# Value products in four parts, and three groups of transposes moved later, in a fused attention and feed-forward kernel

## The reference, cut to what matters

```python
x = x + attn(layernorm(x), ctx, ctx)     # x, ctx: 16 x 256 x 256
x = x + ffn(layernorm(x))

# attn, 8 heads of 32; gates from [q, k, v] @ ifgate_w.T, soft-capped by 15 * tanh(pre / 15)
lf = cumsum(log_sigmoid(f_pre))
log_d = lf[t] - lf[s] + i_pre[s], causal
d = exp(log_d - max_s log_d)
s_mat = (q @ k.T / sqrt(32)) * d
h = (s_mat @ v) / (max(|sum_s s_mat|, exp(-m)) + 5e-5)
h = h * rsqrt(mean(h * h) + 1e-6) * (1 + outnorm_w)

# ffn, ternary weights with a scale for each output
h = silu(x @ w1) * (x @ w2)              # 256 -> 1024
h = gelu(h @ h1); h = gelu(h @ h2)       # 1024 -> 1024, twice
y = h @ w3                               # 1024 -> 256
```

## Time and profile before

| what | value |
|---|---|
| median of 3 runs | 898.24 us (898.09 to 901.56) |
| the profiled execution | 900.49 us |
| its span, first to last instruction | 898.8 us |
| mean granted TensorE clock | 0.929 of 2.4 GHz |
| busy in the span: TensorE products | 827.8 us |
| weight loads | 703.6 us |
| VectorE | 562.0 us |
| ScalarE | 380.5 us |
| GpSimd | 67.1 us |

### The profile page before, as it was taken

The page is one execution under the profiler, slowest core; times in us unless marked ns, Lnnn a source line. Parts: engine busy times, 40 slices in busy tenths (PEclk is TensorE's granted clock), DMA queues, the critical chain, the costliest instruction groups (busy, mean ns, idle before and its releaser), DMA issues.

```text
span 898.8 us, 11800 instructions
## 1 busy us (share of the span) xinstructions
PE 827.8 (92%) x4610; PEld 703.6 (78%) x4610; DVE 562.0 (63%) x1336; ACT 380.5 (42%) x551; POOL 67.1 (7%) x54
## 2 busy tenths in 40 slices
PE   5447799999999999999999999999999999999777
PEld 5347688887887888888887888888888888888566
DVE  4475585847856584848676594848675673655651
ACT  2230362455534472455535462445435551354131
POOL 4240000200020000200020000100020000000000
PEclk7556898999999999999999998999999999999888
DMA  6573100021001300031003100030012100023740
GB/s 243 230 284 128 69 24 25 24 95 71 24 25 60 129 24 25 24 119 47 24 25 117 72 24 25 24 131 35 24 48 95 47 1 1 24 71 113 211 145 25
DMA packets 14635, 66.40 MB, mean 74 GB/s; under 512 B 2032, under 2 KB 2416, under 8 KB 11504
## 3 DMA queue, kind: packets, MB, share of 16 engines
q1 hardware_dynamic: 13280, 54.07, 17.2%
q0 software_dynamic: 1296, 11.53, 3.3%
HBM read 57.08 MB, written 8.52 MB: 73 GB/s over the span
## 4 chain that ended last, share of the span: by engine, by line
PE 53%; DVE 30%; ACT 6%; DMA 5%; issue 4%; POOL 1%; DVEq 0%; ACTq 0%; POOLq 0%
PE ps_f L1129 11%; PE ps_f L1130 10%; DVE decay L735 8%; PE ps_a L1068 7%; PE ps_f L1105 7%; PE ps_f L1106 7%; DMA decay<-w_cols 5%; PE ps_f L1160 3%; PE ps_f L1159 3%; DVE h_lo L844 2%; DVE decay L751 2%; PE ps_a L1049 2%; DVE decay L868 2%; DVE rms L796 2%; DVE stats L646 1%
## 5 line engine op out<-in xcount | busy, mean ns | idle before, releaser
L1129 PE MATMUL ps_f<-h_hi,wgt 128*128 128x512 f32 x1024 | 415.1, 405 | 6.6 <-DVE h_lo L844 6.6
L1130 PE MATMUL ps_f<-h_lo,wgt 128*128 128x512 f32 x1024 | 409.9, 400 | 0.0
L1129 PEld LDWEIGHTS ps_f<-h_hi,wgt 128*128 128x128 f32 x1024 | 199.6, 195 | 51.1 <-DVE h_lo L844 7.7
L1130 PEld LDWEIGHTS ps_f<-h_lo,wgt 128*128 128x128 f32 x1024 | 199.4, 195 | 40.9
L558 ACT ACTIVATE work<-ps_f,scl 128x512 f32<-128x512 f32 x128 | 87.5, 684 | 242.3 <-PE ps_f L1130 242.1
L844 DVE TENSOR_TENSOR h_lo<-work,h_hi 128x512 fp32r<-128x512 f32 x128 | 86.2, 689 | 145.1 <-ACT h_hi L563 144.0
L1105 PE MATMUL ps_f<-h_hi,wgt 128*128 128x512 f32 x256 | 101.4, 396 | 0.0
L1106 PE MATMUL ps_f<-h_lo,wgt 128*128 128x512 f32 x256 | 100.3, 392 | 0.0
L545 ACT ACTIVATE work<-ps_f,scl 128x512 f32<-128x512 f32 x64 | 44.1, 689 | 92.7 <-PE ps_f L1106 92.7
L563 ACT ACTIVATE h_hi<-work 128x512 fp32r<-128x512 f32 x128 | 80.9, 632 | 4.1
L835 DVE SCALAR_TENSOR_TENSOR work<-ps_f,scl,work 128x512 f32<-128x512 f32 x64 | 48.1, 751 | 49.3 <-ACT work L545 49.3
(11 more groups left out here) (148 smaller groups left out, 788.5 us busy)
## 6 DMA issues: line engine op xcount, KB each, us to landing
decay<-m_rows SPq DMA_DIRECT2D x16, 1024.0 KB, 5.9
decay<-w_cols SPq DMA_DIRECT2D x22, 512.0 KB, 4.1
wgt<-w_cols POOLq DMA_DIRECT2D x5, 1024.0 KB, 9.4
v_aug<-ctx_tok SPq DMA_DIRECT2D x8, 528.0 KB, 3.5
z<-x SPq DMA_DIRECT2D x8, 512.0 KB, 4.4
xs<-x SPq DMA_DIRECT2D x8, 512.0 KB, 3.5
wgt<-w_cols POOLq DMA_DIRECT2D x2, 2048.0 KB, 9.6
x_kept<-xs SPq DMA_DIRECT2D x8, 512.0 KB, 2.6
```

What stands on the lines that cost most here:

```text
L1129: pe.matmul(ps_f[:, bank], w, moving(h_hi[layer][:, k], as_is), start=(k == 0), stop=False)
L1130: last = pe.matmul(ps_f[:, bank], w, moving(h_lo[layer][:, k], as_is), start=False, stop=(k == KH - 1))
```

## The change

The value products of each pair are issued in four parts of 16 in place of two of 32, each between big products. The first still follows `make_state` behind group 5. The second comes in the middle of group 6, `read_state` stays behind group 6, the third part comes in the middle of group 7, and the fourth behind k = 0 of groups 0 and 1 of the second hidden layer. `turn_z` goes from between the layers to behind k = 3 of the second, `turn_z2` from behind group 5 to behind group 6, and `turn_rows` from behind group 6 to behind group 7. On ScalarE `take_cols` goes from behind group 6 to behind group 7, and on VectorE `take_num` and `mix_divide` from behind `lo` of group 6 to behind that of group 7. The first pair's attention, ahead of the loop, keeps its order.

```diff
@@ ScalarE, second hidden layer
-                    if g_stage and m == 6:
+                    if g_stage and m == 7:
                         take_cols(g)
@@ VectorE, first hidden layer
                     if a_stage and m == 6:
                         take_far(j)
+                    if a_stage and m == 7:
                         take_num(j)
                         mix_divide(j)
@@ TensorE
-            def values(j, t):
+            def values(j, t, b):
                 if t == 1:
                     pe.wait_ge(s_near, j + 1)
-                for b in range(W):
-                    for h in range(HEADS):
-                        last = pe.matmul(ps_a[:, 2 + b, h * DV:(h + 1) * DV], decay_of(b, h, t), v_aug[:, b * TILES + t, h, :],
-                                         start=True, stop=True)
-                    last.then_inc(s_pv, 1)
+                for h in range(HEADS):
+                    last = pe.matmul(ps_a[:, 2 + b, h * DV:(h + 1) * DV], decay_of(b, h, t), v_aug[:, b * TILES + t, h, :],
+                                     start=True, stop=True)
+                last.then_inc(s_pv, 1)
-            def hidden_layer(i, layer, as_is, after):
+            def hidden_layer(i, layer, as_is, between, within, after):
                 for k in range(KH - 1):
                     for m in range(2):
                         hidden(i, layer, m, (k,), as_is)
+                    between(k)
                 for m in range(2):
                     hidden(i, layer, m, range(KH - 1, KH), as_is)
                     after(m)
                 for m in range(2, KH):
-                    hidden(i, layer, m, range(KH), as_is)
+                    hidden(i, layer, m, range(KH // 2), as_is)
+                    within(m)
+                    hidden(i, layer, m, range(KH // 2, KH), as_is)
                     after(m)
@@ batch
                     if a_stage and m == 5:
                         make_state(j)
-                        values(j, 0)
+                        values(j, 0, 0)
                     if a_stage and m == 6:
                         read_state(j)
-                        values(j, 1)
                 def after_3(m):
                     if g_stage and m == 2:
                         gates(g)
-                    if a_stage and m == 5:
+                    if a_stage and m == 6:
                         turn_z2(j)
-                    if g_stage and m == 6:
+                    if g_stage and m == 7:
                         turn_rows(g)
+                def within_2(m):
+                    if a_stage and m == 6:
+                        values(j, 0, 1)
+                    if a_stage and m == 7:
+                        values(j, 1, 0)
+                def between_3(k):
+                    if a_stage and k == 0:
+                        values(j, 1, 1)
+                    if g_stage and k == 3:
+                        turn_z(g)
-                hidden_layer(i, 0, as_is, after_2)
-                if g_stage:
-                    turn_z(g)
+                hidden_layer(i, 0, as_is, between_2, within_2, after_2)
                 weights_in(pe, 2)
-                hidden_layer(i, 1, as_is, after_3)
+                hidden_layer(i, 1, as_is, between_3, within_3, after_3)
```

More of the change, by code:

```diff
@@ L1204, in after_3, with between_2, within_3 @@
                         count_inexact()
+                def within_2(m):
[3 more added lines that the diff above has]
+                        values(j, 1, 0)
+                def between_2(k):
+                    pass
+                def between_3(k):
[3 more added lines that the diff above has]
+                        turn_z(g)
+                def within_3(m):
+                    pass
                 weights_in(pe, 1)
-                hidden_layer(i, 0, as_is, after_2)
-                if g_stage:
-                    turn_z(g)
+                hidden_layer(i, 0, as_is, between_2, within_2, after_2)
                 weights_in(pe, 2)
-                hidden_layer(i, 1, as_is, after_3)
+                hidden_layer(i, 1, as_is, between_3, within_3, after_3)
                 weights_in(pe, 3)
@@ L1231, in _ @@
             make_state(0)
-            values(0, 0)
+            for b in range(W):
+                values(0, 0, b)
             read_state(0)
-            values(0, 1)
+            for b in range(W):
+                values(0, 1, b)
             turn_rows(1)
```

## The result

The changed kernel takes 876.3 us (875.22 to 878.02, 4 runs) against 898.56 for the kernel before in the same comparison: ratio 0.9754, 95% interval 0.9728 to 0.9781. The forecast was 879.5 (873 to 889). The profiled execution takes 878.02 us with a span of 876.3, 22.5 less than before.

A forecast was written before the change was run, and what follows sets the result against it. TensorE's order was taken to set the loop's time, with clock falls and the rows' wait reachable. 14.4 + 7.7 − 1.9 = 20.2 us took the profile from 900.49 to 880.3; the median forecast was 879.5, range 873 to 889.

The forecast's parts named there:

- Falls of the clock: Nine falls to 1.2 GHz at the loop's blocks of small products; shorter unbroken runs save all 14.4 us.
- The rival's clause: Rival (1): spreading small products doesn't keep the clock up; 892.4 us with all nine falls kept; chance 0.10.
- The wait for the rows: TensorE's wait before `turn_rows`, 1.3 us at most in six batches; all 7.7 us saved.
- VectorE's delay of 2.5 us: Gate rows, ending VectorE's list, come later against T': between −0.6 and +3.2 us, taken as +2.5.
- T': End of the first hidden layer's products on TensorE in the changed kernel; T is the same before.
- Both meetings with GpSimd: VectorE slowed by `split_keys_low` at L784, up to 1.5 us, and by `split_normed_low` at small steps, up to 2.4.
- its upper end of 3.2: Largest delay of the rows against T', 2.3 − 2.95 + 1.5 + 2.4; the wait would still be gone.
- Returns: Changes from small to big products, two becoming five per batch: 3 × 0.09 × 7 = 1.9 us lost.
- Moves at no cost: `turn_z`, `turn_z2`, `take_near`, `take_cols` and queue moves costed at nothing, with cover such as 1.2 us or 3.9 us.
- Sum: 14.4 + 7.7 − 1.9 = 20.2 us saved; profiled execution 900.49 becomes 880.3, median taken as 879.5.
- Rival (2): Another wait replaces the removed one: VectorE's list over 4.2 us late, or gates or `project` wait; 887 us; chance 0.06.

The follow-up runs named there:

- split_alone: Kernel before with both blocks of 32 value products cut in two, 8 big products between, no other move: 884.76 us, ratio 0.9831.
- split_close: Kernel before with value blocks cut in two as halves, but only 2 big products between the parts instead of 8: 896.65 us, ratio 0.9968.
- wide: Kernel before in its own order, each value product moving up to four heads' columns (132) instead of one head's 33: 880.58 us, ratio 0.9787.
- split_rows_late: Kernel before with values cut in two parts, and the gate rows' transposes and copy one group later: 876.24 us, ratio 0.9752.
- rows_late: Kernel before with only the gate rows' transposes and the copy of their result one group later: 890.66 us, ratio 0.9897.
- rows_early: Changed kernel with `turn_rows` and `take_cols` behind group 6 again and `turn_z2` behind group 5: 894.92 us, ratio 0.996.
- the joined run: Changed kernel with its first two value parts joined behind `make_state`, a run of 40 small products again: 878.35 us, ratio 0.9794.

## Why the prediction was right

- **Falls of the clock, 14.4 us.** Right in size: nine falls gone, and split_alone, which does this alone, has a loop 14.65 us shorter, though it pays for two more returns in each batch (0.05). Without these it is 15.0, so a fall cost a little more than the windows had it. The reason was half right. I put it on the length of the unbroken run (2.65 against 4.39 us); split_close has no longer runs than these, and falls worth seven. The rival's clause "nothing shows that only unbroken runs count" was the truer one. The prediction listed the distances of the changed kernel, 8, 8, 8 and 12 big products, and gave them no weight; that they were enough was in part luck. wide shows that at equal lengths and equal distances the products' width decides as well.
- **The wait for the rows, 7.7 us.** Right, and too small. split_alone and split_rows_late differ by the wait alone: 97.68 − 96.16 = 1.52 us in each of six batches, 9.1. The row says 1.29, as it counts from the end of a last product that is modelled at 0.39 us, where the next one would start 0.23 after its start. This is that product in the kernel before:

```profile
386.07 0.39 PE L1130 MATMUL ps_f<-h_lo,wgt 128*128 128x512 f32 x1
```

From 386.07 + 0.23 to 387.75 it is 1.45. The 0.07 between that and the measured 1.52 I can't place.
- **VectorE's delay of 2.5 us.** The rows came at T' + 33.1 against a forecast of T' + 33.0, and TensorE at T' + 34.6 against 34.7. Both meetings with GpSimd took place: L784 lost 1.1 and one small step 2.2 us. With these sizes the prediction's own sum is 2.3 − 2.95 + 1.1 + 2.2 = 2.6, and 33.1 − 30.5 = 2.6 was measured; its upper end of 3.2 had them larger. That the second step would be L797, with one SBUF input, and not another, I hadn't said.
- **Returns, 1.9 us lost.** Too large. The parts' 16 products take 1.70 and not 1.745 us; the weight load of the first starts at 346.62, under the big product before it. By the lengths of batches a return costs 0.03 to 0.06 net. With all three more in each, a batch of the changed kernel takes 96.23 against 96.11 in rows_late without a fall: 0.12, or 0.8 us in all.
- **Moves at no cost.** Right: no wait behind them. But they weren't needed either (split_rows_late), and the later VectorE list that they make costs nothing only because `turn_rows` is moved too (rows_early).
- **Sum.** 15.0 + 9.1 − 0.8 = 23.3, as measured in the loop; 20.2 was forecast. Of the 3.1 between them 1.4 are the rows' wait, 1.1 the returns and 0.6 the falls, all to the same side. The profiled executions are 22.5 apart. From the median the forecast took off 18.7 us (898.24 to 879.5) and not the whole 20.2, in case the median had fewer falls than the profile; the medians are 22.3 apart, so nothing of that shows.
- **Rivals.** Rival (2), the wait that comes back, is what rows_early made: it shows that with `turn_rows` and `turn_z2` in their old places the change would have lost nearly its whole gain.

What stays open: why the clock fell in two of seven batches behind the joined run, where before it was four of seven behind the same run; the runs show such falls in different batches each time, and I made no run that sets their place. It is open too by what means wider products and a larger distance keep the clock up; the runs show only that they do.

## What to carry to other kernels

Lay windows with the granted clock over each block of small products: TensorE can be 100% busy and still be put to 1.2 GHz. Two cures did the same here: parts with enough big products between them, and wider products where the time from start to start stays the same. The wider products need no new order and helped ahead of the loop as well. When a list on another engine is made later by a move, work out where its last link ends against the consumer before leaving the consumer in place; in rows_early a wait of 2.1 us cost 3.1 on average, with the falls behind it.

## What the runs showed of the hardware

- Products of 128x132 in fp32 take the same 0.11 us from start to start as those of 128x33 (`make_state`'s 8 take 0.90 us, and a block of 32, 20 of them with 132 columns, 3.51 against 3.49 us at full clock), so up to 99 columns more were free, and with them the clock didn't fall in seven batches where nine falls had been. Ahead of the loop it rose some 17 us earlier with them.
- At 1.2 GHz the block of 32 products of 128x33 takes 6.7 us (62.39 to 69.08), about twice the 3.49 at full clock: the pace of these products follows the clock too.
- The clock can stay at 1.2 GHz while TensorE is busy without a gap, through 4.00 of 4.00 us in window after window from 64 to 80 us of the changed kernel. The Trainium skill (TensorE: Matmul & The Clock Gate, section "Why this matters for your kernels") asks for no idle gaps between bursts; here TensorE had no gap in the windows with a fall, so the rule alone doesn't keep the clock up.
- The clock fell behind a wait of 2.1 us with ten transposes near it in three of six batches (rows_early), and behind none of 1.3 us (before, split_alone, split_close and wide, six each).
- A one-input VectorE step (L797, 32 elements) took 2.33 us in the median of the changed kernel where it took 0.18 before, and ended with GpSimd's L435, just as the two-input L784 ended with L431. The Trainium skill (SBUF — State Buffer, "Who interferes with whom") allows for that where such a step runs in a mode that uses both ports; no run here shows the mode.
